# Expert heads with slots: expert registers loaded one by one a step ahead, relative attention's gate steps two groups later, three row buffers

## The reference

```python
# L3_attn: 4 x 16 heads, relative attention; the other block, L3_ffn, has 8 heads of 8 experts, top 2
logits = jnp.einsum('bsd,ed->bse', x, w).astype(jnp.float32)
raw = logits.reshape(x.shape[0], x.shape[1], H, E)
vals, idx = jax.lax.top_k(jax.nn.sigmoid(raw), K)
vals = vals / jnp.clip(vals.sum(-1, keepdims=True), 1e-09) * route_scale
gate = (jax.nn.one_hot(idx, E, dtype=vals.dtype) * vals[..., None]).sum(-2)
...
xv = jnp.einsum('bsd,hedp->bshep', x, v_w.reshape(H, E, D, P))
v = jnp.einsum('bshep,bshe->bhsp', xv, gate_v)
att = jax.nn.softmax(jnp.einsum('bhqp,bhkp->bhqk', q, k) * SCALE, axis=-1)
ctx = jnp.einsum('bhqk,bhkp->bqhp', att, v)
out = jnp.einsum('bshep,hepd->bsd', ctx[:, :, :, None, :] * gate_o[..., None], o_w.reshape(H, E, P, D))
```

## Time and profile before

| | |
|---|---|
| median of three runs | 2136.94 us (2129.23 to 2142.82) |
| the profiled execution | 2126.71 us, of which the span 2124.9 us |
| PE busy | 1876.5 us, 88% |
| DVE busy | 1521.2 us, 72% |
| ACT, POOL busy | 974.2 us, 838.5 us |
| relative attention, first scores | 1019.93 us |
| expert heads, first scores | 1373.73 us |

### The profile page before, as it was taken

How to read it: one execution, slowest core, us unless ns; L and a number is a source line. 1 busy time by engine, 2 the same in 40 slices (tenths; PEclk the granted TensorE clock), 3 DMA queues, 4 the chain that set the end, 5 groups by cost and what they waited for, 6 DMA issues and landing times. The chain is left out here.

```text
span 2124.9 us, 32795 instructions
## 1 busy us (share of the span) xinstructions
PE 1876.5 (88%) x9918; PEld 1015.4 (48%) x9918; DVE 1521.2 (72%) x4483; ACT 974.2 (46%) x2257; POOL 838.5 (39%) x1243
## 2 busy tenths in 40 slices
PE   6499998489989958987899999999998999989998
PEld 4233333345555634334566667544444544445543
DVE  6577775567656766997576776478766778767898
ACT  3167765256663426241576777433322333323332
POOL 2556651055542321111376767554231455002341
PEclk9679999589999977999999999999999999999999
DMA  8442222372222029931654565110313223131211
GB/s 277 140 110 34 30 47 37 80 236 54 32 64 47 23 65 149 168 69 48 168 162 148 152 181 162 58 51 34 93 45 86 76 74 93 40 82 38 61 31 30
DMA packets 223059, 189.92 MB, mean 89 GB/s; under 512 B 25605, under 2 KB 206507, under 8 KB 222250
## 3 DMA queue, kind: packets, MB, share of 16 engines
q1 hardware_dynamic: 206842, 163.62, 30.6%
q0 software_dynamic: 15328, 24.10, 4.6%
q10 hardware_dynamic: 720, 0.11, 0.0%
HBM read 112.09 MB, written 75.68 MB: 88 GB/s over the span
## 5 line engine op out<-in xcount | busy, mean ns | idle before, releaser
L2838 DVE SCALAR_TENSOR_TENSOR x<-f_m,f_gs,x 128x128 f32<-128x128 f32 x1024 | 352.7, 347 | 104.5 <-PE f_m L2666 75.5
L512 DVE TENSOR_REDUCE a_nmax<-a_s 128x1 f32<-128x512 f32 (+3 forms) x512 | 278.8, 585 | 125.2 <-PE a_s L323 55.6
L2217 POOL TENSOR_SCALAR a_lg<-a_lg,a_rinv 128x256 f32<-128x256 f32 (+1 forms) x256 | 226.3, 902 | 156.3 <-DVE a_rinv L2254 155.9
L2666 PE MATMUL f_m<-f_wo,f_oT 128*128 128x512 f32 x512 | 263.2, 598 | 3.6 <-DVE x L2838 1.4
L428 ACT ACTIVATE a_pT<-a_st 128x512 f32<-128x512 f32 (+3 forms) x512 | 229.0, 519 | 34.0 <-PE a_st L346 12.2
L2614 POOL DMA_INDIRECT f_yg<-yslot,slot x128 | 121.6, 950 | 279.1 <-PE f_s L2700 217.9
L2838 DVE SCALAR_TENSOR_TENSOR f_val<-f_m,gate,f_val 128x128 f32<-128x128 f32 x448 | 151.7, 343 | 51.1 <-PE f_m L2666 35.6
L323 PE MATMUL a_s<-t_kp,t_qp 96*128 96x512 bf16 (+3 forms) x512 | 166.0, 359 | 10.8 <-DVEq L496 7.6
L346 PE MATMUL a_st<-t_qp,t_kp 99*128 99x512 bf16 (+3 forms) x512 | 163.4, 354 | 1.5 <-ACT a_pT L428 1.2
L2700 PE MATMUL f_s<-xn_pair,f_qT 128*128 128x512 f32 x256 | 135.4, 611 | 30.8 <-issue 24.9
L2791 ACT COPY f_pT<-f_t 128x512 f32<-128x512 f32 x128 | 75.2, 588 | 155.8 <-PE f_t L2708 115.9
(11 more groups left out here) (434 smaller groups left out, 3806.1 us busy)
## 6 DMA issues: line engine op xcount, KB each, us to landing
a_band<-band SPq DMA_DIRECT2D x64, 512.0 KB, 4.6
band<-s_hole SPq DMA_DIRECT2D x16, 1032.0 KB
band<-a_rows SPq DMA_DIRECT2D x64, 256.0 KB, 4.0
yslot<-f_ys SPq DMA_DIRECT2D x36, 256.0 KB, 2.3
w_gate_up<-f_wgu_in SPq DMA_DIRECT2D x4, 1536.0 KB, 17.3
t_qp<-parts SPq DMA_DIRECT2D x192, 32.0 KB
t_kp<-parts SPq DMA_DIRECT2D x192, 32.0 KB
f_xs<-rows SPq DMA_DIRECT2D x6, 832.0 KB, 6.7
```

The source lines that it names most:

```text
L512: v.tensor_reduce(nmax[:, h % 4, qt:qt + 1], s_ps[(b * H * QT + u) % R][:, 0:n], AX.X, ALU.max, negate=True)\
L2217: last = pool.tensor_scalar(lg[:, g % 2, half, p, c0:c0 + n], lg[:, g % 2, half, p, c0:c0 + n], rinv[:, g % 2, p, qt:qt + 1], None, ALU.mult)
L2666: pe.matmul(ps[:, :], left, w, start=True, stop=True).then_inc(full, 1)
L2838: ins = v.scalar_tensor_tensor(out, ps[:, e * P:(e + 1) * P], gate, out, ALU.mult, ALU.add)
```

## The change

Three edits, all for layer 3. The registers of the z fills of step u+1 are loaded in step u, one tile at a time at four places: after the scores, after the first pair of fills, before the second pair, and after it. The four chains of gate steps start at the groups 2, 6, 20 and 24 instead of 0, 4, 18 and 22, and route steps and counting follow two groups later. And there are three row buffers and three slot outputs for the four heads, so that only head 7 uses a buffer again; the third is zeroed in layer 2.

```diff
+            for r in spare_rows:
+                sp.dma_start(r.rearrange("(j p) d -> p j d", p=P), bc(blank[:, :].unsqueeze(1), [P, TILES, P]))\
+                    .then_inc(filled, 16)
+            sp.wait_ge(filled, 16 * (B * 4 + 3))
...
-    CHAINS = {0: (0, 0), 4: (0, 1), 18: (1, 0), 22: (1, 1)}
-    BOTH, COUNT_AT = 2 * GATE, 11
+    CHAINS = {2: (0, 0), 6: (0, 1), 20: (1, 0), 24: (1, 1)}
+    BOTH, COUNT_AT = 2 * GATE, 13
...
-        while room > 0 and waiting and (nth(waiting[0][0]) < 2 or u > opens(SPARSE[nth(waiting[0][0]) - 2])):
+        while room > 0 and waiting and (nth(waiting[0][0]) < 3 or u > opens(SPARSE[nth(waiting[0][0]) - 3])):
...
-                    sp.wait_ge(sent[n % 2], 16 * 2 * NT * (n // 2 + 1))
+                    sp.wait_ge(sent[n % 3], 16 * 2 * NT * (n // 3 + 1))
...
+                    if j == 0 and nth(h) >= 3:
+                        sp.wait_ge(combined, NT * (nth(h) - 2))
...
-                if i == 0 and c == 0 and n >= 2:
+                if i == 0 and c == 0 and n >= 3:
                     for s in xs_in:
-                        pool.wait_ge(s, 16 * (n - 1))
-                pool.indirect_dma_start(rows[n % 2], place_of(c, i, h), k.xn[:, i, :], None).then_inc(sent[n % 2], 16)
+                        pool.wait_ge(s, 16 * (n - 2))
+                pool.indirect_dma_start(rows[n % 3], place_of(c, i, h), k.xn[:, i, :], None).then_inc(sent[n % 3], 16)
...
-            def owners(names):
-                for kind, h, j in names:
+            def owners(u, quarter):
+                for kind, h, j in slots.get(u, []):
                     if kind == "z":
-                        for t in tiles_of(j):
+                        for t in tiles_of(j)[quarter:quarter + 1]:
                             expert[h, t] = pe.value_load(k.owner[0:1, h, t:t + 1], min_val=0, max_val=(E - 1) * P)
...
-                owners(slots[u])
                 if u < UNITS:
                     scores(u)
+                owners(u + 1, 0)
...
                 fill(pairs[u][0])
+                owners(u + 1, 1)
                 slot_fill(slots[u][0:1])
                 if 1 <= u <= UNITS:
                     turn(u - 1)
                 if turned_at(u) is not None:
                     values(turned_at(u))
+                owners(u + 1, 2)
                 for pair in pairs[u][1:]:
                     fill(pair)
+                owners(u + 1, 3)
                 slot_fill(slots[u][1:])
```

More of the change, by code:

```diff
@@ L1402, in _ @@
                              bc(hole[:, :].unsqueeze(1), [P, 4 * QT, HOLE])).then_inc(filled, 16)
-            sp.dma_start(spare_rows.rearrange("(j p) d -> p j d", p=P), bc(blank[:, :].unsqueeze(1), [P, TILES, P]))\
-                .then_inc(filled, 16)
-            sp.wait_ge(filled, 16 * (B * 4 + 2))
+            for r in spare_rows:
+                sp.dma_start(r.rearrange("(j p) d -> p j d", p=P), bc(blank[:, :].unsqueeze(1), [P, TILES, P]))\
+                    .then_inc(filled, 16)
+            sp.wait_ge(filled, 16 * (B * 4 + 3))
         @block.tensor
@@ L1869, in relative_heads @@
     CUTS = (0, 5, 10, 15, GATE)
-    CHAINS = {0: (0, 0), 4: (0, 1), 18: (1, 0), 22: (1, 1)}
-    BOTH, COUNT_AT = 2 * GATE, 11
+    CHAINS = {2: (0, 0), 6: (0, 1), 20: (1, 0), 24: (1, 1)}
+    BOTH, COUNT_AT = 2 * GATE, 13
     COUNTED = BOTH + 1 + NT
-    ROUTE = {8: (0, 6), 9: (6, 12), 10: (12, 1 + NT), 12: (20, 22), 13: (22, 27), 14: (27, 29), 15: (29, 31), 16: (31, 33),
-             17: (33, 33 + ROUTES)}
+    ROUTE = {10: (0, 6), 11: (6, 12), 12: (12, 1 + NT), 14: (20, 22), 15: (22, 27), 16: (27, 29), 17: (29, 31), 18: (31, 33),
+             19: (33, 33 + ROUTES)}
     CHAIN_START = {(0, 0): 0, (0, 1): GATE, (1, 0): BOTH + 1 + NT + 13 + ROUTES, (1, 1): BOTH + 1 + NT + 13 + ROUTES + GATE}
@@ L2520, in switch_heads @@
         wv_in = k.f3_wv_in + [ph.sem("wv_in2")]
-        yslot = [nc.dram_tensor(f"yslot{i}", (TILES * P, P), F32, kind="Internal").ap() for i in range(2)]
+        yslot = [nc.dram_tensor(f"yslot{i}", (TILES * P, P), F32, kind="Internal").ap() for i in range(3)]
         fold = ph.sb("fold", [P, H, P])
@@ L2541, in switch_heads @@
         m_free = [ph.sem(f"m_free{i}") for i in range(4)]
-        wo_in, sent, got = ([ph.sem(f"{n}{i}") for i in range(2)] for n in ("wo_in", "sent", "got"))
+        wo_in, got = ([ph.sem(f"{n}{i}") for i in range(2)] for n in ("wo_in", "got"))
+        sent = [ph.sem(f"sent{i}") for i in range(3)]
         xs_in = [ph.sem(f"xs_in{i}") for i in range(3)]
@@ L2578, in _ @@
                             filled("x", SPARSE[n - 1], (CHUNK * (c + 1) - 1) // 4)
-                        sp.dma_start(xs[:, CHUNK * c:CHUNK * (c + 1), :], rows[n % 2][CHUNK * P * c:CHUNK * P * (c + 1), :]
+                        sp.dma_start(xs[:, CHUNK * c:CHUNK * (c + 1), :], rows[n % 3][CHUNK * P * c:CHUNK * P * (c + 1), :]
                                      .rearrange("(j p) d -> p j d", p=P)).then_inc(xs_in[c], 16)
@@ L2584, in _ @@
                     n = len(tiles_of(j))
-                    sp.dma_start(yslot[nth(h) % 2][4 * P * j:4 * P * j + n * P, :].rearrange("(j p) d -> p j d", p=P),
+                    if j == 0 and nth(h) >= 3:
+                        sp.wait_ge(combined, NT * (nth(h) - 2))
+                    sp.dma_start(yslot[nth(h) % 3][4 * P * j:4 * P * j + n * P, :].rearrange("(j p) d -> p j d", p=P),
                                  ys[:, index(h, j) % RING, 0:n * P].rearrange("p (j d) -> p j d", d=P))\
@@ L2613, in gather @@
                 for c in range(2):
-                    pool.indirect_dma_start(yg[:, n % 2, c, i, :], None, yslot[nth(h) % 2], place_of(c, b * QT + i, h))\
+                    pool.indirect_dma_start(yg[:, n % 2, c, i, :], None, yslot[nth(h) % 3], place_of(c, b * QT + i, h))\
                         .then_inc(got[n % 2], 16)
@@ L3104, in program @@
             band = nc.dram_tensor("band", (P + B * 16 * T * 257,), F32, kind="Internal").ap()
-            spare_rows = nc.dram_tensor("spare_rows", (TILES * P, P), F32, kind="Internal").ap()
+            spare_rows = [nc.dram_tensor(f"spare_rows{i}", (TILES * P, P), F32, kind="Internal").ap() for i in range(2)]
             norm_and_logits(nc, k, "n2", d["f2_wr"], 8, early=early)
@@ L3109, in program @@
         Phase.retire(nc)
-        layer3(nc, k, d, band, (rows, spare_rows), out)
+        layer3(nc, k, d, band, (rows, *spare_rows), out)
 def laid_out(a):
```

## The result

The changed kernel takes 2084.61 us (median; 2080.66 to 2086.88), the kernel before 2136.94 us (2129.23 to 2142.82): a ratio of 0.9755, with an interval of [0.972, 0.9791]. It is faster, by 52 us where 29 were forecast, and outside the forecast's range. The two profiled executions are 2126.71 and 2080.66 us: 46.05 us less.

What follows compares the result with a forecast made beforehand. PE was taken to bound the kernel, idling before the scores behind register loads. Gains of 23.6 (loads), 6 (buffers) and 0 us made 29.6, rounded 29: from the median 2136.94 to 2108 us, range 2098 to 2123.

Steps and rivals of the forecast that it cites:

- The bound and the place: Expert heads with slots, layer 3: PE bounds; it idles before the scores behind bursts of register loads, 28.1 us.
- from the last load to the next product: Burst of four before the scores: 0.33 us of its 2.96 us of issue, on top of 0.66 us a load.
- register loads: Expert heads, layer 3: moving 156 loads removes gaps before the scores; 23.6 us gained, ends 14 and 28.
- 3 us returned to DVE: Expert heads: with the gaps cut, PE waits more for DVE; 3 us taken back, ends 0 and 14.
- 1.5 us behind turns: Third load of a step, behind a turn of 0.67 us: 0.3 us shows if the turn was waited for; 1.5 us lost.
- 2.6 us left with ACT f_prob: Three gaps before the scores where the exponentials came last: 2.6 us expected to stay.
- three row buffers: Steps 60 to 63 and 68 to 71: no scatters between gathers any more, 6 us gained, ends 3 and 7.
- The combine on DVE is in order ahead of the next maxima, so ACT, the turn and PE wait: Around step 60: gathers made late by scatters hold the combine, and PE waits 3.16 us.
- the gathers stay late: Steps 60 and 68: gathers wait for scores and an earlier combine, so buffers bring nothing; gain 23, 2114 us; chance 0.08.
- Zero fill and gate steps: Third buffer's zero fill hidden, 0 us; relative attention's gate steps two groups later, 0 us, ends -1 and +1.
- The slow one: Rival: each register load cuts PE's look-ahead, 0.33 us showing at all 156 loads; 17 us slower, 2154 us; chance 0.05.
- The price of 0.6 us for a lone load: Rival: a lone load takes 607 ns, needing 1.30 us of stock; up to 25 us come back, 2128 us; chance 0.03.

Runs made afterwards that it cites:

- the repeat of the kernel before: The kernel before run and traced once more with no edit: 2114.07 us, ratio 1.0005.
- The longer bursts: The whole change with bursts of 6 to 13 further register loads ahead of the scores of eight dense-head steps (9 to 23): 2116.96 us, one run.

## Why the prediction was wrong, step by step

**The bound and the place were right.** The 28.1 us of gap in the earlier trace rows is gone, as 156 loads of 300 ns stay. That a burst is priced against the stock, 2.96 us against 1.24, holds in kind in every run: single loads hide, two at a place partly show, four together show unless the stock is larger, as in the earlier trace rows.

**One reading in it was wrong.** The 0.33 us "from the last load to the next product" are the last load's own register operation and assertion, which the 0.66 us a load has in it already. What made that burst long is a load of 0.60 us among the four:

```profile
L2672 PEldq TENSOR_LOAD <-owner x4: 296/338/602, 1520.2 to 1522.2; - x4
```

The row of 13 above gives 0.65 us a load and nothing besides. So a lone load needs 0.65 us of stock, not 0.99, and a burst of four 2.6. The gaps of 3.4 us, ahead of the steps 39 and 87, are no bursts of four either. Those steps have two z fills, and seven loads stood in a row:

```profile
L2672 PEldq TENSOR_LOAD <-owner x7: 296/300/309, 1613.0 to 1616.9; - x7
```

**The term "register loads" was mis-sized: 23.6 us forecast, 40.1 measured** (39.1 against the repeat of the kernel before, on other chips). This is the step that failed: the path was right, and the size of the term was not. It was off at four points:

- *3 us returned to DVE.* Nothing was. The fills' wait for DVE fell, from 1.1 to 0.8 us. The ratio 0.76 of the earlier trace rows already said so; the 0.45 us waits that I took as signs of a bound were each paid inside the stock.
- *1.5 us behind turns.* Nothing, by the kernel without loads. The 0.99 us that it was worked out from is 0.65, which the 0.67 us of a turn cover.
- *2.6 us left with ACT f_prob* in the earlier trace rows. These gaps went with the others. They stand in the repeat of the kernel before too, and with the loads edit alone, the same exponentials in place, they don't. So the burst was in them, and the profile had put a wait of two causes down to the one that came last. With each register loaded twice, 1.4 us of it came back. PE's waits for ACT in the repeat, then in the loads edit alone:

```profile
PE f_s L2700 <- ACT f_prob L2798: 2.8, 4, 1.2
...
PE f_t L2708 <- ACT f_prob L2798: 1.0, 3, 0.4
```

```profile
PE f_t L2708 <- ACT f_prob L2801: 1.1, 3, 0.4
```

- *Gaps priced at their length.* With the three points above the sum is 30.7 us, and the idle time that went is 31.54; the other 8.6 us are busy time of PE behind the gaps. I had priced none of it. Of this, 3.4 us are clock: steps 39 and 87 stand behind the two gaps of 3.4 us, first in the kernel before:

```profile
1617.52:1625.41 7.89, 7.89 (x29) 4.64 (x30) 3.85 (x12) 1.64 (x4) 0.00 (x0) 0.81 1.21 298
1900.28:1908.37 8.09, 8.09 (x29) 4.57 (x29) 3.85 (x12) 1.63 (x4) 0.00 (x0) 0.79 1.19 297
```

then in the changed kernel:

```profile
1601.73:1608.02 6.29, 6.29 (x30) 3.89 (x29) 5.66 (x19) 1.63 (x4) 2.87 (x3) 1.00 0.83 235
1860.44:1866.72 6.28, 6.28 (x29) 3.88 (x28) 5.65 (x19) 1.63 (x4) 0.00 (x0) 1.00 0.89 229
```

The longer bursts made such losses anew. The second share is that of the restart. Step 26 went from 7.51 to 5.62 us, 1.89 for a gap of 1.73, so 0.16 us more, and the first product behind the gap takes 1.12 us against 1.02, so that step 27 is some 0.10 us shorter too. That is 0.26 us a gap, and 17 gaps over 1 us give 4.4. The longer bursts show the same two amounts behind the gap of 2.11 us: step 12 took 2.27 us more, step 13 0.10. The last 0.8 us can't be placed.

**The term "three row buffers" had a wrong mechanism: 6 us forecast, 0 measured** ([0.9983, 1.0009] alone). The earlier trace rows are real, but the step "The combine on DVE is in order ahead of the next maxima, so ACT, the turn and PE wait" was never followed up: ACT's own timeline has its input ready at 1732.93 and the copy at 1738.20. The number came out right in the first pair of traces (6.11 us) by luck, for the wrong reason. The rival "the gathers stay late" had the right price for this term, 0, and the wrong reason too, since they weren't late at all.

**Zero fill and gate steps: 0 forecast, 0 measured** (ratio 0.9997 for the gate steps, the fill inside the 0.9996 of the buffers).

**The other rivals.** None came. The slow one, a price of 0.22 us on each load, would be 34 us; the kernel without loads is 1.6 us faster. The price of 0.6 us for a lone load isn't seen either: the longest of 156 is 706 ns, the middle one 300. The Trainium skill, DMA: Bandwidth & Descriptors, latency and other measured facts, puts the floor of a `tensor_load` at about 600 ns; the trace disagrees.

**What remains of the 52 us.** The loads edit alone came to ratios of 0.983 and 0.980 on two chips, the whole change to 0.980 on two: some 37 to 43 us. The first comparison is larger because its four runs of the kernel before lie about 22 us above the 2112.6 to 2115.5 us of all four later jobs, and those of the changed kernel only 13 us above its later ones. The stall of ACT and the slower steps 0 to 23 are parts of this that a trace shows; the rest stays open. I forecast from that median, and could not have known. Even so the step above stays wrong: 39 to 40 us were there, and 23.6 forecast.

## What to carry to other kernels

Price work on an in-order sequencer against what it has already handed over at that point: the stock lasts from the start of that work to the end of the last product handed over. Spread the loads so that each place needs less than that; loads with only a pair of products between them are still a burst. A gap on the bottleneck costs more than its length (the restart, and behind the longer ones the clock), and a wait there that the profile puts down to a neighbour may go with the gap itself. Before a wait is blamed on an order of work, follow it to the engine that stood still, and see whether a second execution has it at all.

## What the runs showed of the hardware

- ACT stood still for 5.3 us with its input ready (the rows above), and again for 4.0 us, in one of two traces of the same program. Unexplained.
- A register load held PE's sequencer for 0.65 us (13 in a row: 8.4 us), of which the load itself is 0.30. The stock of products was 1.24 us behind a bank just freed, 1.8 us behind a slot fill and the scores, and 2.7 or 3.2 us in dense steps.
- A gap cost PE 0.26 us beyond its length, without any change of the clock.
- Behind a gap of 3.4 to 3.5 us steps 39 and 87 lost 1.6 to 1.8 us to the clock in both traces of the kernel before, and 3.1 us in both steps of the kernel with the buffers alone, whose order of work on PE is the same (row below: 9.43 us, granted clock 0.67, against 7.89 at 0.81). So neither the length of the gap nor PE's order of work alone gives the loss. And behind the transfer's wait of 1.5 to 2.1 us at step 72 the granted clock fell (0.93 over steps 72 to 75) in 4 of the 15 traces that have that wait.

```profile
1605.76:1615.19 9.43, 9.43 (x29) 5.38 (x29) 3.94 (x12) 1.63 (x4) 2.87 (x3) 0.67 1.14 289
```
